# A cross-attention and mixture-of-experts kernel, rebuilt around a streamed dispatch

## What is computed

```python
x = x + align(ctx, layernorm(x))        # per sample
x = x + ffn(layernorm(x))

def align(small, large):                # 77 rows against 1024 rows
    D = sqrt(max(aa + bb - 2 * small @ large.T, 0))
    # R[i, j] = D[i, j] + min(R[i-1, j], R[i, j-1], R[i-1, j-1])
    # walk back from the last corner to the first along the smallest neighbour
    # each row j of the result is the sum of the rows small[i] on that path

def ffn(x):                             # 4096 rows
    scores = softmax(x @ gate_w.T)      # 16 experts in 4 groups
    # with gate_b added: keep the 2 best groups, in them the 2 best experts
    h = silu(x @ We1[e] + be1[e]) * (x @ We3[e] + be3[e])        # 128 wide
    y = sum over the 2 experts of weight * (h @ We2[e] + be2[e])
    z = silu(x @ ws1 + bs1) * (x @ ws3 + bs3) @ ws2 + bs2         # shared, 256 wide
    return y + z
```

## Time and profile before

| | us |
|---|---|
| runs | 580.51, 582.17, 585.84 |
| median | 582.17 |
| span of the profiled execution | 585.5 |
| the run nearest to it | 585.84 |
| busy in the span: PE, DVE, ACT, POOL | 315.1, 400.4, 164.7, 168.3 |
| mean granted clock of PE | 0.795 of full |

### The profile page before, as it was taken

The page is one execution under the profiler, slowest core; times in us unless marked ns, Lnnn a source line. Parts: engine busy times, 40 slices in busy tenths (PEclk is TensorE's granted clock), DMA queues, the critical chain, the costliest instruction groups (busy, mean ns, idle before and its releaser), DMA issues.

```text
span 585.5 us, 9525 instructions
## 1 busy us (share of the span) xinstructions
PE 315.1 (54%) x1851; PEld 210.9 (36%) x1853; DVE 400.4 (68%) x2103; ACT 164.7 (28%) x447; POOL 168.3 (29%) x197
## 2 busy tenths in 40 slices
PE   1275000000000078889688579757999999899200
PEld 1264000000000045433244345445777777677100
DVE  3877889999999928668795035054666566566297
ACT  1355400000000012476313356132444444344100
POOL 1216000000000001120037747741555555455300
PEclk9988555555555577798799989968999999999755
DMA  8200389999950020000018512312554443343399
GB/s 326 109 2 3 84 269 316 228 217 216 223 186 1 1 83 1 0 1 1 0 45 263 222 55 99 109 63 86 151 156 139 141 145 118 123 130 116 112 389 360
DMA packets 48864, 77.44 MB, mean 132 GB/s; under 512 B 7030, under 2 KB 39100, under 8 KB 46783
## 3 DMA queue, kind: packets, MB, share of 16 engines
q1 hardware_dynamic: 41568, 59.92, 35.7%
q0 software_dynamic: 6912, 16.83, 8.2%
q10 hardware_dynamic: 351, 0.33, 0.2%
HBM read 41.50 MB, written 37.64 MB: 135 GB/s over the span
## 4 chain that ended last, share of the span: by engine, by line
DVE 36%; PE 36%; DMA 9%; ACT 6%; issue 4%; another core or an unknown queue 4%; POOL 3%; SPq 0%; DVEq 0%; POOLq 0%; ACTq 0%
PE psT L822 12%; PE psT L832 7%; DVE xk L1266 4%; DVE V L1030 4%; PE psD L809 4%; DVE R L998 3%; PE psT L766 3%; DMA slot_rows<-stage,slot 3%; DVE carry L1036 3%; POOL slot_rows L470 2%; DVE carry L1004 2%; DVE mask L1026 2%; PE psC L707 2%; DVE A L1037 2%
## 5 line engine op out<-in xcount | busy, mean ns | idle before, releaser
L478 POOL DMA_INDIRECT results<-ys,idx x80 | 78.7, 984 | 76.0 <-issue 48.6
L648 PE MATMUL psT<-onesb 128*128 128x512 bf16 x24 | 8.0, 503 | 152.9 <-DVE mask L1026 152.9
L822 PE MATMUL psT<-w,xsT 128*128 x320 | 84.7, 388 | 0.0
L470 POOL DMA_INDIRECT slot_rows<-stage,slot x64 | 62.9, 983 | 67.9 <-DVE slot L1187 36.0
L766 PE MATMUL psT<-x2T,sw 128*128 128x512 f32 x128 | 61.2, 630 | 18.3 <-DVE silu L1079 16.6
L461 POOL TENSOR_SCALAR x2n<-xk,sm 128x256 f32<-128x256 f32 x16 | 9.0, 564 | 201.5 <-DVE sm L1061 190.3
L648 PEld LDWEIGHTS psT<-onesb 128*128 128x128 bf16 x24 | 2.9, 125 | 157.5 <-issue 156.4
L822 PEld LDWEIGHTS psT<-w,xsT 128*128 128x128 f32 x320 | 55.5, 194 | 6.1 <-issue 1.5
L1236 DVE TENSOR_TENSOR ys<-psT,b 128x256 f32<-128x256 f32 x80 | 34.0, 425 | 32.7 <-issue 19.0
L832 PE MATMUL psT<-w,hgT 128*128 x160 | 52.4, 409 | 5.7 <-ACT hgT L617 5.3
L1254 DVE TENSOR_TENSOR hb<-psT,b 128x256 f32<-128x256 f32 x80 | 34.0, 425 | 26.0 <-PE psT L822 15.3
(11 more groups left out here) (190 smaller groups left out, 693.3 us busy)
## 6 DMA issues: line engine op xcount, KB each, us to landing
slot_rows<-fill SPq DMA_DIRECT2D x80, 128.5 KB, 7.8
xs<-slot_rows SPq DMA_DIRECT2D x80, 128.5 KB
xk<-in_x SPq DMA_DIRECT2D x8, 1024.0 KB, 11.9
back<-results SPq DMA_DIRECT2D x8, 1024.0 KB, 8.4
out<-xk SPq DMA_DIRECT2D x8, 512.0 KB, 8.7
w<-in_L_ffn_We SPq DMA_DIRECT2D x1, 2048.0 KB, 14.4
b<-in_L_ffn_be SPq DMA_DIRECT2D x2, 1024.0 KB
b<-in_L_ffn_be SPq DMA_DIRECT2D x1, 2048.0 KB
```

The costliest lines, as they stand in the source:

```text
L470: pool.indirect_dma_start(out=slot_rows, out_offset=bass.IndirectOffsetOnAxis(ap=slot[:, w, T:T + 1], axis=0), in_=stage[:, T % STAGES, w, ...
L478: pool.indirect_dma_start(out=results, out_offset=bass.IndirectOffsetOnAxis(ap=idx[:, u:u + 1], axis=0), in_=ys[:, u, :], in_offset=None, ...
L822: mm = pe.matmul(psH[c % 2], xsT[:, c % 2, k, :], w13f[:, bass.ds(k * E * 2 * I + e, 2 * I)], start=(k == 0), stop=(k == KC - 1))
```

## The change

Nearly every stage is written anew.

*Front.* PE turns raw x; the distances are scaled and shifted afterwards, half of the columns by ACT, half by DVE. The inverse square root comes from logarithm and exponential alone, and three parts (rows 0 to 15, 16 to 39, 40 to 76) replace two. *Alignment.* The scans start from a constant; the shuffle writes into the row that the scan reads. V is bf16. *Mask.* Written in four pieces; rows 36 to 76 come back early, rows 0 to 35 at the end on the queues of SP and ACT. The logits of x are computed under the alignment and carried as 17 more columns (gate and mean) through `gather`. *Dispatch.* Routing in four groups of eight tiles. Each expert has a region of its own in `slot_rows`, so that a row's place is known before the counts are; a table `rowtab` names the first row of each of 79 tiles, 16 short transfers fill the ends of the regions. Every tile has its own `stage`, which both scatters and `turn2` read. POOL scatters group after group and waits at 41 of its 64 scatters for a signal of PE (`gathered_by` to `z_by`). Six chunks of the shared part (`h`; five of `z`) run beside it. *Expert loop.* PE multiplies the expert's weights as the stationary operand, so that h comes out turned; a copy of the weights, four deep, is made by ACT and DVE; biases ride in ACT's silu and in DVE's product; eight input buffers. *Tail.* SP reads `results` when the tiles that hold real rows have landed; ACT scales rows for DVE in five groups and two halves; two shared chunks run here.

The diff, cut to its core:

```diff
-PARTS = (slice(0, CUT), slice(CUT, CTX))
+PARTS = ((0, CUT), (CUT, 40), (40, CTX))
...
-SLOT_TILES = 80
-SLOTS = SLOT_TILES * P
...
+SLOT_TILES = (2 * TOK + E * (P - 1)) // P
...
+EARLY = 5
+AHEAD = 1
...
+            for part, lo in enumerate(MASK_CUTS):
+                hi = NT if part == 0 else MASK_CUTS[part - 1]
                 sp.wait_ge(mask_ready, part + 1)
                 sp.dma_start(mask_skew[:, lo * CH:hi * CH], mask[:, lo:hi, :].rearrange("p t w -> p (t w)")
                              ).then_inc(mask_out, 16)
...
+            sp.wait_ge(fill_rows_ready, 1)
+            for e in range(E):
+                sp.reg_load(sp_row[e % 4], fill_row[0:1, e:e + 1])
+                at = sp.snap(sp_row[e % 4], min_val=e * RG, max_val=e * RG + TOK)
+                sp.dma_start(slot_rows[bass.ds(at, P), :], fill[:, :]).then_inc(filled, 16)
...
+            need = [sp.value_load(landed[0:1, u:u + 1], min_val=16 * (TOK * 2 // P // 8), max_val=16 * 10)
+                    for u in range(8)]
             for u in range(8):
-                sp.wait_ge(res_out[u], 16 * (SLOT_TILES // 8))
+                sp.wait_ge(res_out[u], need[u])
+
             def load_results(g):
-                sp.dma_start(back[:, g % 4, :, :, :], results_in[:, 4 * g:4 * g + 4, :, :]).then_inc(tail_in[g % 4], 16)
-
+                sp.dma_start(back[g][:, :, :, :], results_in[:, 4 * g:4 * g + 4, :, :]).then_inc(tail_in[g], 16)
+
+            sp.wait_ge(h_ready, 2 * EARLY)
             for g in range(4):
                 load_results(g)
...
+            sp.wait_ge(y_done, SLOT_TILES)
+            for g in range(4, 8):
+                load_results(g)
+            for g in range(7):
                 sp.wait_ge(combined, g + 1)
-                if g + 4 < 8:
-                    load_results(g + 4)
...
+            gathered_by = {1: 15, 2: 17, 3: 18, 5: 20, 14: 23, 16: 25, 17: 26, 21: 28, 30: 30, 31: 31, 32: 32}
+            turned_by = {6: 5, 8: 6, 10: 7, 12: 8, 22: 9, 23: 10, 25: 11, 27: 12, 36: 13, 38: 14, 39: 15, 41: 16}
+            ranked_by = {13: 2, 29: 3, 43: 4}
+            h_by = {9: 1, 28: 4, 42: 6, 47: 7, 48: 8, 54: 9, 56: 10, 62: 11}
+            z_by = {19: 1, 34: 3, 35: 4, 50: 5, 51: 6, 58: 7, 60: 8}
+
             for T in range(TILES):
-                if T % HT == 0:
-                    pool.wait_ge(routed, T // HT + 1)
-                pool.wait_ge(staged, T + 1)
+                if T % GT == 0:
+                    pool.wait_ge(routed, T // GT + 1)
+                    pool.wait_ge(staged, T + GT)
                 for w in range(2):
+                    k = 2 * T + w
+                    if k in gathered_by:
+                        pool.wait_ge(gathered, gathered_by[k])
+                    if k in turned_by:
...
+                    if k in z_by:
+                        pool.wait_ge(z_ready, z_by[k])
                     pool.indirect_dma_start(
                         out=slot_rows, out_offset=bass.IndirectOffsetOnAxis(ap=slot[:, w, T:T + 1], axis=0),
-                        in_=stage[:, T % STAGES, w, :], in_offset=None).then_inc(scattered[T % STAGES], 16)
+                        in_=stage[:, T, :], in_offset=None).then_inc(scattered[T % GT // (GT - LAG)], 16)
+
+            def send(i, u):
+                pool.wait_ge(y_read, 8 * i + u + 1)
+                if not isinstance(i, int) or 8 * i + u + 4 <= SLOT_TILES:
+                    pool.wait_ge(h_done, 8 * i + u + 4)
+                pool.sem_inc(passed, 1)
+                pool.indirect_dma_start(
+                    out=results, out_offset=bass.IndirectOffsetOnAxis(ap=idx[:, u:u + 1], axis=0),
+                    in_=ys(u), in_offset=None, bounds_check=DUMP - 1,
+                    oob_is_err=False).then_inc(res_out[u], 16)

...
+                act.wait_ge(dist_ready, n + 1)
+                act.wait_ge(norm_ready, n // 4 + 1)
+                for k in range(4 * n, 4 * n + 4):
+                    ins = act.activation(cost[:, :, 1 + k], psD[n % 2][:, k % 4, 0:CTX], ACT.Identity,
+                                         scale=sm[:, 1, k:k + 1], bias=sm[:, 9, k:k + 1])
+                ins.then_inc(dist_act, 1)
...
+                if live(i, c + 2):
+                    load_expert(act, act_expert, i, c + 2)
+                    e = expert(act, act_expert, c + 2)
+                    if not head(i, c - 2):
+                        act.wait_ge(h_done, q - 1)
+                    act.activation(w_now[:, (c + 2) % 4, 1, :], w13f[:, bass.ds(E * WD + e, 2 * I)],
+                                   ACT.Copy).then_inc(w_act, 1)
+                    act.wait_ge(x_turned, q + 3)
+                    act.activation(xsT[:, (c + 2) % 4, :, :].rearrange("p c t -> p (c t)"),
+                                   psX[c % 2], ACT.Copy).then_inc(xT_copied, 1)
+                if live(i, c):
+                    e = expert(act, act_expert, c)
+                    act.wait_ge(h_done, q + 1)
+                    if not head(i, c - 2):
+                        act.wait_ge(gated, q - 1)
+                    act.activation(sg[:, c % 2, :], psH[c % 4][:, 0:P], ACT.Silu,
+                                   bias=w13f[:, bass.ds(e + D, 1)]).then_inc(silu_done, 1)
+
...
+            def scale_rows(g, *ws):
+                act.wait_ge(tail_in[g], 16)
+                for w in ws:
+                    for T in range(4 * g, 4 * g + 4):
+                        ins = act.activation(back[g][:, T % 4, w, :], back[g][:, T % 4, w, :], ACT.Copy,
+                                             scale=wt[:, w, T:T + 1])
+                    ins.then_inc(scaled_rows, 1)
...
-                        mm = pe.transpose(psX[r % 2][:, k * P:(k + 1) * P], xs[:, r % 4, k * P:(k + 1) * P], ident[:, :])
+                        mm = pe.transpose(psX[r % 2][:, k * P:(k + 1) * P], xs[:, r % 8, k * P:(k + 1) * P], ident[:, :])
                     mm.then_inc(x_turned, 1)
-                if live(i, c - 2):
-                    pe.wait_ge(gated, q - 1)
+                if live(i, c):
+                    pe.wait_ge(xT_copied, q + 1)
+                    pe.wait_ge(w_act, q + 1)
+                    pe.wait_ge(w_dve, q + 1)
                     if not head(i, c - 4):
-                        pe.wait_ge(hgT_copied, q - 3)
-                    pe.transpose(psG[c % 2], hg[:, c % 2, :], ident[:, :]).then_inc(g_turned, 1)
-                if live(i, c):
-                    e = expert(pe, pe_expert, c)
-                    pe.wait_ge(xT_copied, q + 1)
-                    if not head(i, c - 2):
-                        pe.wait_ge(hb_ready, q - 1)
-                    for k in range(KC):
-                        mm = pe.matmul(psH[c % 2], xsT[:, c % 2, k, :], w13f[:, bass.ds(k * E * 2 * I + e, 2 * I)],
-                                       start=(k == 0), stop=(k == KC - 1))
+                        pe.wait_ge(gated, q - 3)
+                    for lo in (0, I):
+                        for k in range(KC):
+                            mm = pe.matmul(psH[c % 4][:, lo:lo + P], w_now[:, c % 4, k, lo:lo + I],
+                                           xsT[:, c % 4, k, :], start=(k == 0), stop=(k == KC - 1))
...
+            def refine(part):
+                lo, hi = PARTS[part]
+                c, r, d, i = (m[:, lo:hi, 1:W] for m in (cost, root, rest, inv))
+                if part == 0:
+                    dve.wait_ge(clipped, 1)
+                dve.wait_ge(inverted, part + 1)
+                link(dve.tensor_tensor(r, c, i, ALU.mult))
+                link(dve.scalar_tensor_tensor(out=d, in0=r, scalar=-0.5, in1=i, op0=ALU.mult, op1=ALU.mult))
+                dve.scalar_tensor_tensor(out=c, in0=d, scalar=1.5, in1=r, op0=ALU.add,
+                                         op1=ALU.mult).then_inc(cost_ready[part], 1)
+
+            clip(0)
+            clip(1)
+            refine(0)
+            clip(2)
+            refine(1)
+            refine(2)
+
...
-                start(dve.tensor_tensor_scan(R[:, t + 1, :], M[:, t, :], cst[:, t, :], carry[:, t:t + 1],
+                start(dve.tensor_tensor_scan(R[:, t + 1, :], M[:, t, :], cst[:, t, :], BIG,
...
-                start(dve.tensor_tensor_scan(rev(V, t), rev(cst, t), rev(A, t + 1), carry[:, t + 1:t + 2],
+                start(dve.tensor_tensor_scan(rev(V, t), rev(cst, t), rev(A, t + 1), 1.0,
...
+                if live(i, c + 2):
+                    load_expert(dve, dve_expert, i, c + 2)
+                    e = expert(dve, dve_expert, c + 2)
+                    if not head(i, c - 2):
+                        dve.wait_ge(h_done, q - 1)
+                    dve.tensor_copy(w_now[:, (c + 2) % 4, 0, :], w13f[:, bass.ds(e, 2 * I)]).then_inc(w_dve, 1)
...
+                    dve.scalar_tensor_tensor(out=idx[:, c % 8:c % 8 + 1], in0=xs[:, c % 8, D + 1:ROW],
+                                             scalar=rowf[:, bass.ds(q, 1)], in1=xs[:, c % 8, D:D + 1],
+                                             op0=ALU.not_equal, op1=ALU.add).then_inc(id_copied, 1)
...
```

(15 more changed lines are left out.)

1477 lines of the change are left out of this document (865 added, 612 removed).

## The result

The changed kernel takes 483.97 us (median of 6 runs, 483.12 to 485.48), the kernel before 582.4 beside it. The ratio is 0.8295, 95% interval 0.8266 to 0.8323. The forecast was 465, the range 440 to 508. So the side and the range held, but the case that I had called likeliest (452 to 478) did not.

The account below looks back on a forecast made before the run. Alignment was taken as DVE-bound (98%), the loop as PE-bound (96%), the middle as a chain with no engine over 77%. Front 45, alignment 120, middle 130, loop 137.5 and tail 33 sum to 465.5; forecast 465, range 440 to 508.

Parts of the forecast that it names:

- the case that I had called likeliest: Whole kernel: the sum of the stages comes out as forecast, 452 to 478 us; chance 0.60.
- Alignment: Alignment steps: scans starting from a constant save 0.06 us a step, taking the stage from 135.0 to 120 us.
- Front: Start to first alignment step: turning raw x and scaling distances afterwards takes it from 70.7 to 45 us.
- the bound of 52: Front's upper bound in us, for PE running at half clock in its short bursts.
- Middle: Last alignment step to first expert tile: overlapped group dispatch, ending with PE's three chunks, takes 193.5 to 130 us.
- clock and waits: Middle: 6 us added on top of the landing and load, to reach 130.
- Loop: Expert loop: 79 tiles at 1.66 us plus 6 for fill and drain, from 148.6 to 137.5 us.
- Tail: After the loop: earlier result fetch, DVE's 29 us of work and last store, 37.7 to 33; bound 40 if ACT's scalings are late.
- Late signals: Rival, middle: TensorE's signals held while POOL issues; 41 stops of 1 us make the whole 506; chance 0.15.
- The port: Rival, loop: DVE's weight copies and POOL's sends block each other, loop 180 us, whole 508; chance 0.06.
- no overlap: Rival, middle: groups wait for each other in a ring, the stage stays 193 us, whole 528; chance 0.04.
- better: Rival: dispatch groups of 18 us, middle 115 and front 43, whole 448; chance 0.14.

Follow-up runs that it names:

- e1: Changed kernel with each scan's start read from a column in memory, not a constant: 466.7 us on a chip where the kernel before takes 568.9.
- e4: Changed kernel with the wait for h of four tiles later taken out of GpSimd's send: 452.1 us where the kernel before takes 568.9.
- e7: Changed kernel fetching expert results only after all 79 tiles have landed, not just the real ones: 493.7 us where the kernel before takes 583.5.
- e8: Changed kernel without the scatter queue's 41 waits for TensorE, the send's wait for h kept: 503.1 us where the kernel before takes 583.2.
- e5: Changed kernel without both the scatter queue's 41 waits for TensorE and the send's wait for h: 510.6 us where the kernel before takes 583.5.
- e9: Changed kernel with loop results written by SP's plain DMA, GpSimd idle there, experts' results left out of the sum: 475.2 us where the kernel before takes 583.2.
- e2: Changed kernel without the scatter queue's 41 waits for TensorE, the send's wait for h kept: 452.0 us where the kernel before takes 568.9.
- e6: Changed kernel with both halves of the expert's weights copied by VectorE, none by ScalarE: 481.8 us where the kernel before takes 583.5.
- e10: Changed kernel with TensorE turning three tiles ahead, silu and product a tile later, y three tiles after h: 491.0 us where before takes 583.2.

## Why the prediction was right, and where it was not

**Alignment.** Right in size and reason: 120.8 for 120, 228 ns for 225, and e1 takes the one cause away and back.

**Front.** 48.7 for 45. The refinement after the last squared column took 14.1 (34.0 to 48.1), forecast 13.8, with a slip in it: seven operations on 512 numbers at the rate of that row are 4.0, not 4.6, and took 4.8. What was missed is before it: the last four squared columns wait 4.1 us for PE's distances (done at 34.0, not 31). That isn't the clock, which the bound of 52 was for: it is granted in full (1.00) from 20 to 33.3, and the 0.86 of the stage comes from the stretch behind, where PE has nothing to do. PE stands for 1.2 us before its last six products, for a cause that the profile doesn't name.

**Middle.** 129.1 for 130, and its marks too: first scatter +29.4 (forecast 30), fourth group ranked at +91 (93), PE's three chunks done at +124.9 (124). Yet the step that was to set the end, PE's chunks, does not: PE waits from there to +129.1 for the first tile's rows. The forecast had POOL done at +111 and it was done at +123.7, 12.8 of that by stops at the ties, which were 1.5 in e1 on the prompt chip. Without them (e4, on that chip) the middle is 117.9. So this term came out right because the 6 us put on for "clock and waits" and a queue that I took for slack happened to meet: two misses that cancel.

**Loop.** The step that failed: "with the old overhead (1.78 - 1.61 = 0.17) I take 1.66". PE's own pace is 1.53 to 1.55, not 1.50, and the overhead is no constant of the loop: it is 0 where signals are prompt (119.1 over 78 tiles, 1.53) and some 0.27 where they are late (1.80). The value taken lies between two states of which each run is in one. That accounts for 9.9 of the 16.8.

**Tail.** DVE's work was sized right in sum (28.2 busy, forecast 29), though the parts listed add to 26.9 and the two adds of a group took 2.48 us, not 2.2. The cause of the end was wrong: ACT's scalings, which the forecast had only in its bound of 40, and the landing that they wait for, set it (e7). 36.3 for 33.

**Late signals.** The rival had the mechanism (e8, e5) and was given 0.15; the measured 484 lies between it (506) and the likeliest case. It had place and sign wrong. The 41 ties were priced as 41 stops that cost 1 us each; they cost 10 to 13 in all, and without them the scatters take 20 longer. The larger loss, 17 to 21 us, is in the loop (121.7 in e9 and 119.1 in e4 for 138.9 and 140.3), which I had not looked at for this, though GpSimd issues there for 0.98 of every 1.5 us. Nor does a signal have to wait for the end of a long run, as the prediction had it (e8). In all, the change gains 98 us on a chip with late signals and some 115 (568.9 to an estimated 454) on one without.

**The port, no overlap, better.** The port falls as a price: copies are held beside sends, but for at most 0.3 us each and 2.7 in all. The earlier trace rows could not show it, for that operation starts 0.42 us after its scatter, and the copies held start 0.52 to 0.80 after a send. No overlap is refuted by the scatters, which begin 29.4 us after the last step, not 94.5. The case called better, 448, is what e2 and e4 nearly reached on the chip with prompt signals: the middle near to it (117.9 for 115), the front not (49.5 for 43), and a loop of 126.1 for 137.5 that makes up for it.

Of what the prediction said to look for: no "remote" wait over 2 us was wrong (5.3 on ACT, 5.0 on DVE), PE above 90% was right (92%) and told nothing of the stumbles; the copies on DVE took 0.33 on average, not under 0.3, since some are held (e6); PE's clock was 0.90 to 0.93 of full until 260, not at its full level from the first shared chunk on; POOL's idle of 31.7 stayed under 35, and 1.80 a tile is just the bound that I had named for being wrong.

## What to carry to other kernels

Where GpSimd issues indirect DMAs without pause, look at how long after TensorE's end the other engines start; if it is 2 us and more, give the queue a wait on TensorE's progress at the points where others need it, and price the queue's rhythm before its length. More slack between engines is no cure by itself, if it undoes that pacing (e10). Before a difference of 3% between two variants is explained, run the unchanged one beside them: here one and the same text (e2 and e8) took 452.0 us on one chip and 503.1 on another.
